# One relative-position bank for both axes, and tokens stored in row-pair order, in a two-layer windowed attention kernel

## The reference, cut to what matters

```python
x = x + conv0(_gn(x), ...)            # _gn: group norm over the image, 32 groups
x = x + conv1(_gn(x), ...)
# each layer:
qkv = x.reshape(B, 196, C) @ qkv_w + qkv_b
rel_h = jnp.einsum('bhwc,hkc->bhwk', q4, Rh)     # q4 = q as (B*nh, 14, 14, 16)
rel_w = jnp.einsum('bhwc,wkc->bhwk', q4, Rw)
attn = q @ k.T * scale + rel_h[..., :, None] + rel_w[..., None, :]
out = softmax(attn) @ v
return out @ proj_w + proj_b
```

## Time and profile before

| | |
|---|---|
| median of three runs | 2332.41 us |
| the profiled execution | 2339.97 us, span of its instructions 2338.2 us |
| TensorE matmul | 2094.7 us, 90% of the span, 27904 records |
| TensorE weight load | 1595.9 us, 68% |
| VectorE | 1653.4 us, 71% |
| ScalarE | 1621.4 us, 69% |
| GpSimd | 714.4 us, 31% |
| granted TensorE clock, mean | 0.978 of 2.4 GHz |

### The profile page before, as it was taken

How to read it: one execution, slowest core, us unless ns; L and a number is a source line. 1 busy time by engine, 2 the same in 40 slices (tenths; PEclk the granted TensorE clock), 3 DMA queues, 4 the chain that set the end, 5 groups by cost and what they waited for, 6 DMA issues and landing times.

```text
span 2338.2 us, 73485 instructions
## 1 busy us (share of the span) xinstructions
PE 2094.7 (90%) x27904; PEld 1595.9 (68%) x27904; DVE 1653.4 (71%) x3923; ACT 1621.4 (69%) x3713; POOL 714.4 (31%) x1796
## 2 busy tenths in 40 slices
PE   1899999999999989999999999899989999999998
PEld 1677676776767767667667766677766766777765
DVE  5677777667767677777677777677767777777675
ACT  0577777677767667767676777677767776777675
POOL 1233323333333233333233333233223333333230
PEclk9899999999999999999999999999999999999999
DMA  1333434333434333433333443344334343334331
GB/s 47 84 94 95 104 91 105 91 92 91 103 93 97 90 94 93 101 93 93 91 98 91 94 103 96 88 96 100 91 91 102 94 100 93 94 93 103 91 92 47
DMA packets 170550, 216.34 MB, mean 93 GB/s; under 512 B 29783, under 2 KB 138072, under 8 KB 170202
## 3 DMA queue, kind: packets, MB, share of 16 engines
q1 hardware_dynamic: 170202, 211.64, 37.7%
HBM read 117.00 MB, written 57.80 MB: 75 GB/s over the span
## 4 chain that ended last, share of the span: by engine, by line
PE 39%; DMA 33%; SPq 14%; DVE 6%; issue 4%; ACT 3%; POOL 1%; POOLq 0%; ACTq 0%; DVEq 0%
PE ps_m L412 18%; DMA q_st<-mrow 17%; DMA k_dram<-qk_hl 10%; PE ps_sc L538 7%; PE ps_max L525 6%; SPq L375 6%; DMA q_dram<-qk_hl 6%; DVE qk_hl L734 4%; PE ps_o L557 3%; SPq L382 3%; ACT qk_hl L598 2%; SPq L341 2%; SPq L387 2%; PE ps_m L501 2%; DVE rel_hl L776 1%
## 5 line engine op out<-in xcount | busy, mean ns | idle before, releaser
L722 DVE TENSOR_REDUCE mx<-ps_max 98x2 f32<-98x392 f32 x1536 | 819.4, 562 | 232.6 <-PE ps_max L525 215.5
L586 ACT ACTIVATE probs<-ps_sc 98x392 f32<-98x392 f32 x1536 | 714.5, 497 | 232.3 <-PE ps_sc L538 198.2
L525 PE MATMUL ps_max<-k_st,q_st 124*98 124x196 f16 x3072 | 548.9, 261 | 82.4 <-DVE mx L722 82.1
L538 PE MATMUL ps_sc<-q_st,k_st 125*98 125x196 f16 x3072 | 523.3, 252 | 95.6 <-DMA q_st<-mrow 94.1
L776 DVE TENSOR_TENSOR rel_hl<-ps_m,rel_hi 64x504 f16<-64x504 f32 (+1 forms) x768 | 431.4, 562 | 162.0 <-ACT rel_hi L643 152.9
L525 PEld LDWEIGHTS ps_max<-k_st,q_st 124*98 124x98 f16 x3072 | 295.0, 126 | 296.4 <-issue 198.0
L538 PEld LDWEIGHTS ps_sc<-q_st,k_st 125*98 125x98 f16 x3072 | 320.9, 126 | 123.1 <-DMA q_st<-mrow 120.4
L557 PE MATMUL ps_o<-probs,v_st 98*32 98x196 f32 x6144 | 389.6, 340 | 0.5 <-ACT o_sb L578 0.5
L634 ACT ACTIVATE rel_hi<-ps_m,is_lo 64x504 f16<-64x504 f32 (+1 forms) x384 | 223.9, 583 | 189.1 <-PE ps_m L471 185.7
L471 PE MATMUL ps_m<-q_st,rel_st 64*32 64x84 f16 x7168 | 341.6, 266 | 4.8 <-DVE rel_hl L776 4.5
L809 POOL TENSOR_TENSOR msq<-mv 96x2 f32<-96x2 f32 x128 | 24.4, 191 | 1007.1 <-DVE mv L748 1007.1
(11 more groups left out here) (72 smaller groups left out, 3293.8 us busy)
## 6 DMA issues: line engine op xcount, KB each, us to landing
q_st<-q_dram SPq DMA_DIRECT2D x128, 294.0 KB, 3.8
k_st<-k_dram SPq DMA_DIRECT2D x256, 147.0 KB, 3.9
q_dram<-qk_hl SPq DMA_DIRECT2D x128, 147.0 KB, 2.6
k_dram<-qk_hl SPq DMA_DIRECT2D x128, 147.0 KB, 2.7
q_st<-rel_hl SPq DMA_DIRECT2D x256, 73.5 KB
q_st<-rel_hl SPq DMA_DIRECT2D x256, 64.3 KB
xa<-in_x SPq DMA_DIRECT2D x64, 147.0 KB
xd<-in_x SPq DMA_DIRECT2D x64, 147.0 KB
```

The costliest lines, as they stand in the source:

```text
L525: last = nc.tensor.matmul(ps_max[head % 2][0:HT, h * TOK:h * TOK + TOK], q_st[u.r][0:R_MAX, head, h, :], k_st[u.r][0:R_MAX, head, :], star ...
L538: last = nc.tensor.matmul(ps_sc[head % 2][0:HT, kt * TOK:kt * TOK + TOK], k_st[u.r][0:STACK, head, kt * HT:kt * HT + HT], q_st[u.r][0:STAC ...
L586: nc.scalar.activation(probs[head][:, :, :], ps_sc[head % 2][0:HT, 0:2 * TOK].rearrange("p (k t) -> p k t", k=2), ACT.Exp, scale=1.0 / (QS ...
L722: nc.vector.reduce_max(mx[u.r % 2][:, head, :], ps_max[head % 2][0:HT, 0:2 * TOK].rearrange("p (q k) -> p q k", q=2), axis=AX.X).then_inc( ...
```

## The change: what it does

A token's place in an image is no longer 14 * row + column. Rows go in pairs, and within a pair the tokens stand column by column: both tokens of column 0, both of column 1, and so on (in the code, axes k, b, r: pair, column, row in the pair). The order is made by ScalarE when it copies the transposed input to `xT`, undone when it copies the attention's result to `o_sb`, and given once to the constant rows, by one VectorE copy to a new tile `oh_f16` from which the 48 copies then read.

A rel bank now holds, for both axes, the tokens of its own rows (six, six and two). For axis 0 there is still one matmul per row and half. For axis 1 every bank needs all 14 columns, each with only the bank's rows: 28 matmuls per bank. All four quarters of a bank then have the same layout, and one instruction of 128 partitions on ScalarE and one on VectorE take it (`rel_views` goes, `rel_part` and `rel_bank` come).

```diff
-        def rel_views(dst, ps, n, a0):
-            by_row = (dst[0:64, :, a0 * SIDE:(a0 + n) * SIDE],
-                      ps[0:64, 0:n * HH * SIDE].rearrange("p (h x) -> p h x", h=HH))
-            by_col = (dst[64:128, :, :].rearrange("p h (a b) -> p (h a) b", a=SIDE)[:, :, a0:a0 + n],
-                      ps[64:128, 0:n * HH * SIDE].rearrange("p (x b) -> p x b", b=n))
+        def rel_part(dst, n):
+            a0 = sum(RELB[:n])
+            return dst[:, :, a0 * SIDE:(a0 + RELB[n]) * SIDE]
+        def rel_bank(n):
+            return ps_m[BANK[f"rel{n}"]][:, 0:RELB[n] * HH * SIDE].rearrange("p (h x) -> p h x", h=HH)
...
-                    for i in range(rows):
-                        a = sum(RELB[:n]) + i
-                        for axis in range(2):
-                            w = 2 * (SIDE - 1 - a)
+                    a0 = sum(RELB[:n])
+                    for i in range(SIDE):
+                        for axis in range(2) if i < rows else (1,):
+                            w = 2 * (SIDE - 1 - (i if axis else a0 + i))
                             for half in range(2):
+                                p = 64 * axis + 32 * half
+                                to = ps[p:p + RW, 0:rows * HH * SIDE].rearrange("p (h t) -> p h t", h=HH)\
+                                    .rearrange("p h (k b r) -> p h k b r", r=2, b=SIDE)
                                 q = q_st[u.r][0:R_REL, half * HH:half * HH + HH, :, :]\
-                                    .rearrange("p h q t -> p h (q t)")
...
+                                    .rearrange("p h q t -> p h (q t)")[:, :, a0 * SIDE:(a0 + rows) * SIDE]\
+                                    .rearrange("p h (k b r) -> p h k b r", r=2, b=SIDE)
                                 if axis == 0:
-                                    to = to.rearrange("p (h a b) -> p h a b", h=HH, a=rows)[:, :, i, :]
+                                    to, q = (part[:, :, i // 2, :, i % 2] for part in (to, q))
                                 else:
-                                    to = to.rearrange("p (x b) -> p x b", b=rows)[:, :, i]
+                                    to, q = (part[:, :, :, i, :] for part in (to, q))
...
-                            nc.scalar.copy(o_sb[u.r % 2][:, g, :], ps_o[:, 0:TOK]).then_inc(s_o, 1)
+                            nc.scalar.copy(o_sb[u.r % 2][:, g, :].rearrange("p (k r b) -> p k r b", r=2, b=SIDE),
+                                           ps_o[:, 0:TOK].rearrange("p (k b r) -> p k r b", r=2, b=SIDE))\
+                              .then_inc(s_o, 1)
...
-                        nc.scalar.copy(xT[u.r % 2][:, :, :],
+                        nc.scalar.copy(xT[u.r % 2][:, :, :].rearrange("p c (k b r) -> p (c k) b r", r=2, b=SIDE),
...
-                            dst, src = rel_views(rel_hi[u.r % 2], ps_m[BANK[f"rel{n}"]], RELB[n], sum(RELB[:n]))[0]
-                            nc.scalar.activation(dst, src, ACT.Identity, scale=is_lo[0:64, 0:1])
-                            dst, src = rel_views(rel_hi[u.r % 2], ps_m[BANK[f"rel{n}"]], RELB[n], sum(RELB[:n]))[1]
-                            nc.scalar.activation(dst, src, ACT.Identity, scale=is_lo[64:128, 0:1])\
-                              .then_inc(s_rhi, 1)
+                            nc.scalar.activation(rel_part(rel_hi[u.r % 2], n), rel_bank(n), ACT.Identity,
+                                                 scale=is_lo[:, 0:1]).then_inc(s_rhi, 1)
...
+            nc.vector.tensor_copy(oh_f16[R_REL:STACK, :].rearrange("p (k b r) -> p k r b", r=2, b=SIDE),
+                                  oh_raw[R_REL:STACK, :].rearrange("p (k r b) -> p k r b", r=2, b=SIDE)).then_inc(s_oh, 1)
...
-                    nc.vector.tensor_copy(k_st[i][R_REL:STACK, head, :], oh_raw[R_REL:STACK, :])
+                    nc.vector.tensor_copy(k_st[i][R_REL:STACK, head, :], oh_f16[R_REL:STACK, :])
...
-                            for (h, src), (l, _) in zip(hi, lo):
-                                last = nc.vector.tensor_tensor(l, src, h, ALU.subtract)
-                            last.then_inc(s_rlo, 1)
+                            nc.vector.tensor_tensor(rel_part(rel_hl[u.r % 2], n), rel_bank(n),
+                                                    rel_part(rel_hi[u.r % 2], n), ALU.subtract).then_inc(s_rlo, 1)
```

More of the change, by code:

```diff
@@ L456, in job @@
                     bank_free(pe, unit, name)
[L458 to L461 removed]
+                    a0 = sum(RELB[:n])
+                    for i in range(SIDE):
+                        for axis in range(2) if i < rows else (1,):
+                            w = 2 * (SIDE - 1 - (i if axis else a0 + i))
                             for half in range(2):
+                                p = 64 * axis + 32 * half
+                                to = ps[p:p + RW, 0:rows * HH * SIDE].rearrange("p (h t) -> p h t", h=HH)\
+                                    .rearrange("p h (k b r) -> p h k b r", r=2, b=SIDE)
                                 q = q_st[u.r][0:R_REL, half * HH:half * HH + HH, :, :]\
[L464 to L466 removed]
+                                    .rearrange("p h q t -> p h (q t)")[:, :, a0 * SIDE:(a0 + rows) * SIDE]\
+                                    .rearrange("p h (k b r) -> p h k b r", r=2, b=SIDE)
                                 if axis == 0:
[L468 removed]
+                                    to, q = (part[:, :, i // 2, :, i % 2] for part in (to, q))
                                 else:
[L470 to L474 removed]
+                                    to, q = (part[:, :, :, i, :] for part in (to, q))
+                                last = nc.tensor.matmul(to, rel_st[:, lay, axis, w:w + RW], q, start=True, stop=True)
                     last.then_inc(s_rel_ps, 1)
@@ L632, in iteration @@
                                 wait_dma(act, s_rel, b4, 4)
-                            dst, src = rel_views(rel_hi[u.r % 2], ps_m[BANK[f"rel{n}"]], RELB[n], sum(RELB[:n]))[0]
-                            nc.scalar.activation(dst, src, ACT.Identity, scale=is_lo[0:64, 0:1])
-                    for n in range(len(RELB)):
-                        u = due(unit, s, AT[f"rel{n}"] + ACT_LATER["rel"])
-                        if u:
-                            act.wait_ge(s_rel_ps, u.n * 3 + n + 1)
-                            b4 = unit((AT["rel0"] + ACT_LATER["rel"]) // HEADS + 2)
-                            if n == 0 and active(b4):
-                                wait_dma(act, s_rel, b4, 4)
-                            dst, src = rel_views(rel_hi[u.r % 2], ps_m[BANK[f"rel{n}"]], RELB[n], sum(RELB[:n]))[1]
-                            nc.scalar.activation(dst, src, ACT.Identity, scale=is_lo[64:128, 0:1])\
-                              .then_inc(s_rhi, 1)
+                            nc.scalar.activation(rel_part(rel_hi[u.r % 2], n), rel_bank(n), ACT.Identity,
+                                                 scale=is_lo[:, 0:1]).then_inc(s_rhi, 1)
                     u = due(unit, s, AT["v"] + ACT_LATER["v"])
@@ L771, in iteration @@
                                 wait_dma(dve, s_rel, b4, 4)
-                            hi, lo = (rel_views(part[u.r % 2], ps_m[BANK[f"rel{n}"]], RELB[n], sum(RELB[:n]))
-                                      for part in (rel_hi, rel_hl))
                             dve.wait_ge(s_rhi, u.n * 3 + n + 1)
-                            for (h, src), (l, _) in zip(hi, lo):
-                                last = nc.vector.tensor_tensor(l, src, h, ALU.subtract)
-                            last.then_inc(s_rlo, 1)
+                            nc.vector.tensor_tensor(rel_part(rel_hl[u.r % 2], n), rel_bank(n),
+                                                    rel_part(rel_hi[u.r % 2], n), ALU.subtract).then_inc(s_rlo, 1)
                     u = due(unit, s, AT["oT"] + DVE_LATER["oT"])
```

13 lines of the change are left out of this document (5 added, 8 removed).

## The result

The changed kernel takes 2538.09 us (median of four runs, 2525.18 to 2559.78), the kernel before on the same chip 2330.77 us (2325.98 to 2334.24): 1.09 times as long, 95% interval 1.0809 to 1.0992. Forecast were 2423 us, in a range of 2318 to 2480. The direction was right and the size was not: +207 us instead of +91. Two executions, both of the kernel that B calls `after, 42`, ran at a lower granted clock from their start to their end (2131 us at 0.853, 6068 us at 0.341) and stand in no median or ratio here.

A forecast was written before the change was run, and what follows sets the result against it. The unit was taken as set by the 10.9 us leg from q's and k's copies to the maxima's landing, plus slots 10 to 3. 55 more drops at 1.7 us (+94) and the start (-3) gave 2423 us, range 2318 to 2480.

The forecast's parts named there:

- The bound and the leg: Leg from q's and k's copies to the maxima's landing, 10.9 us, plus slots 10 to 3 sets the unit; leg unchanged.
- 0.33 us off each of `rel0` and `rel1`: Rel jobs in slots 5 and 6: each falls from 1.03 to 0.70 us, together saving 0.66 us a unit.
- 0.29 for `rel2`: Rel job in slot 8: grows from 0.41 to 0.70 us, adding 0.29 us a unit.
- The slot-8 wait: TensorE's wait for VectorE's reduction goes because copies and remainders are halved: 0.64 us a unit.
- the shortest shown: Rel jobs: axis 0's interval between pairs, 0.042 us, taken for axis 1's 14 pairs, giving 0.70 us a job.
- The classes from the trace of before: Slot-10 waits grouped by length with a drop share each; longer waits give some 71 drops instead of 16.
- The price of a drop: Each fall of TensorE's clock behind the slot-10 wait costs 1.7 us; 55 more give +94 us.
- Rival 2: Slot-10 wait takes up the gain and the clock does not care: 2329 us; chance 0.13.
- rival 3: Denser rel jobs keep TensorE's clock up, so the drops go: 2299 us; chance 0.16.
- Rival 1: Rel banks stay as slow through axis 0's stepped writes, only the slot-8 wait goes: 2385 us; chance 0.16.
- More than forecast: Rel jobs at their fast bound, units wait near 3 us, some 115 drop: 2488 us; chance 0.55 together with the forecast.
- The start: VectorE's 48 setup copies, 8.43 us, get shorter from 16-bit data: -3 us, bounds 0 to -6.

The follow-up runs named there:

- B: Experiments sending the second half's maxima earlier in SP's order, in the changed kernel and in the kernel before; measured times from 2026.91 to 2254.77 us.
- after, 42: Changed kernel with the second half's maxima sent ahead of k's two loads on SP; 2026.91 us in its second run, ratio 0.8674.
- before + 5: Kernel before with five unread 1 KB transfers added on SP ahead of the maxima; 2634.51 us, ratio 1.1256.
- before + 9: Kernel before with nine unread 1 KB transfers added on SP ahead of the maxima; 3007.88 us, ratio 1.285.
- after + 3: Changed kernel with three unread 1 KB transfers added on SP ahead of the maxima; 2675.25 us, ratio 1.1474.
- after, 43: Changed kernel with the second half's maxima sent ahead of the residual's load and the image's store, still behind k's loads; 2254.77 us, ratio 0.9653.
- E: Two variants of the kernel before: axis 1 of the rel jobs reading packed (2467.57 us) or writing packed (2346.86 us).

## Why the prediction was wrong in size

**The bound and the leg: right.** The unit was set by the leg and by slots 10 to 3. The leg was forecast to stay at 10.9 us; it went from 10.80 to 10.72 on average. Everything saved inside it came back as waiting, the rel lines have 0.3% of the chain, and the copies' 420 us were worth nothing here. B shows the same from the other side: with the leg shortened below TensorE's work the change pays.

**The terms of the sum: too small.** I took 0.33 us off each of `rel0` and `rel1`; it was 0.44 and 0.42. I added 0.29 for `rel2`; it was 0.04. The slot-8 wait gave its 0.64. By these rows 1.46 us went, by the means of the unit 1.62 (9.88 to 8.26 us of work in slots 3 to 10), forecast 1.01. The mis-sized step was the interval between pairs, "the shortest shown" (0.042 us): pairs of 36 columns begin 0.035 us apart, and those of 12 columns, by the 0.45 us of `rel2`, (0.45 - 0.11) / 14 = 0.024. That left a wait of 2.46 us instead of 2.0. The classes from the trace of before held on these longer waits: low stretches behind 22 of 34 waits from 1.5 to 2.0 us, 25 of 29 from 2.0 to 2.5, 48 of 52 above (forecast 0.6 for the first and 0.95 above 2.0). With the right wait they would have given the right number: 43 x 0.6 + 24 x 0.95 + 55 x 0.95 = 101 of 122 units. It was 97 in 117, 81 more than before instead of 55.

**The price of a drop: the step that failed.** I wrote "A longer wait holds more of the low stretch, so I price a drop at 1.7". The first half is true, and the conclusion does not follow: when the fall comes inside the wait, the lower clock lasts a second stretch, which lies wholly over work that is on the chain. Measured in the same manner (growth of slots 10 to 3 over growth of the count): (8.50 - 6.81) x 117 / 81 = 2.44 us in the kernel after, and (7.89 - 6.81) x 117 / 75 = 1.69 with five transfers, where nearly all are single. So 1.7 was right for a single stretch. By parts, for the 117 units: 94 us forecast, 26 more drops at 1.7 are 44, and 0.74 more for each of 81 is 60; together 198, less 117 x 0.08 = 9 for the leg: 189, and 188 in the table of the units. The price is an average over the kernel and not measured drop by drop. The four doubles among 16 in the trace of before (units of 19.96 us on average, singles 18.97, none 17.35) could have warned me; I averaged over them.

A better unit of account is the time at the lower clock. Against the kernel before, each us of it adds to slots 10 to 3: 0.39 (after), 0.45 (before + 5), 0.41 (before + 9), 0.36 (after + 3), 0.40 (after, 43, with 1.49 us at the lower clock a unit). It is under the half that a clock of 0.50 would cost; part of each stretch lies over the wait, where it costs nothing.

**The rivals.** Rival 2 (the clock doesn't care) and rival 3 (the clock rises) fell: 0.879. Rival 1 had the cause partly right. Axis 0's pairs, which now write every second word, did slow down, to 0.072 us from about 0.04. In E stepped writing alone costs that; but axis 0 now also reads every second element, and no run takes the two apart. Only six pairs do it, and the slow reading, which was twice as dear, is gone. The Trainium skill, PSUM — Partial Sum Buffer, Specifications (TRN2), has non-contiguous patterns in PSUM slow matmuls significantly; the runs of E agree and put a number to it, about double for words 24 bytes apart. "More than forecast" (case 4, 2488 us) was the right direction, and its reason holds for the smaller part: the faster jobs account for the 44 us above, the length of the stretches for the 60. `rel_hl` did not get in the way of the maxima (3.98 us to land in the unit shown, before 3.85, and the leg did not grow).

The clock: low stretches stood behind 47 of 63 waits from 1.5 to 2.5 us in the kernel after. The Trainium skill, TensorE: Matmul & The Clock Gate, HAM oscillation, ties them to longer pauses than these; the measurement decides against it, since nearly all of these would then stay at the full clock.

**The start.** The 48 copies took 5.99 us and the one that feeds them 0.39, before 8.43: -2.0 us, forecast -3. The rows, in order of time:

```profile
7.03 0.39 DVE L670 CAST oh_f<-oh_raw 61x196 f16<-61x196 f32 x1
7.45 5.99 DVE L675 COPY k_st<-oh_f 61x196 f16<-61x196 f16 x48
```

## What to carry to other kernels

Work that is taken off an engine inside a leg that doesn't contain it is not worth nothing: on TensorE it can be worth less than nothing, because the longer wait lowers the clock for the work behind it, which is on the chain. So first shorten the leg (here the maxima sent before k's two loads and two more issues, worth 2336.73 - 2199.35 = 137 us by itself, 2341.26 - 2026.91 = 314 with the change), then the work. If the leg can't be shortened, useless matmuls right ahead of the wait buy the clock back, where it falls often: in the kernel before, with 16 low stretches, 8 of them gained nothing. And when low stretches are counted in a trace, their length is counted too, not the number alone.
